# Second cross attention of a Perceiver block: where head values, output product and absorbed queries stand in a round

## What is computed

```python
def _L1_xattn_ref(x, context, Wq, Wk, Wv, Wo, bo):
...
    B, Sq, _ = x.shape
    h, d = (HEADS, DIM_HEAD)
    scale = d ** (-0.5)
    q = (x @ Wq).reshape(B, Sq, h, d).transpose(0, 2, 1, 3)
    k = (context @ Wk).reshape(B, -1, h, d).transpose(0, 2, 1, 3)
    v = (context @ Wv).reshape(B, -1, h, d).transpose(0, 2, 1, 3)
    scores = jnp.einsum('bhid,bhjd->bhij', q, k) * scale
    attn = jax.nn.softmax(scores, axis=-1)
    out = jnp.einsum('bhij,bhjd->bhid', attn, v)
    out = out.transpose(0, 2, 1, 3).reshape(B, Sq, h * d)
    return out @ Wo + bo
...
x = x + _L1_xattn_ref(_layernorm(x, axis=-1), ctx_768, L1_xattn_Wq, L1_xattn_Wk, L1_xattn_Wv, L1_xattn_Wo, L1_xattn_bo)
```

## Time and profile before

| | us |
|---|---|
| three executions | 2245.73, 2248.62 (median), 2255.6 |
| the profiled execution | 2261.09 |
| its span, first to last instruction | 2259.3 |
| mean granted clock of PE, of 2.4 GHz | 0.905 |
| second cross attention, rounds | some 1008 to 1788 |

### The profile page before, as it was taken

The page is one execution under the profiler, slowest core; times in us unless marked ns, Lnnn a source line. Parts: engine busy times, 40 slices in busy tenths (PEclk is TensorE's granted clock), DMA queues, the critical chain, the costliest instruction groups (busy, mean ns, idle before and its releaser), DMA issues.

```text
span 2259.3 us, 43825 instructions
## 1 busy us (share of the span) xinstructions
PE 2044.9 (91%) x17873; PEld 1683.2 (75%) x17873; DVE 1324.7 (59%) x2900; ACT 923.9 (41%) x1868; POOL 651.6 (29%) x674
## 2 busy tenths in 40 slices
PE   6999999999995887759999999999999899879994
PEld 4777777777774776659898988989889667646663
DVE  5787777877877555437564755756455245532222
ACT  4666666666554333524343433434333221102221
POOL 4444444444434220233232323323231000020002
PEclk9999999999997989779899998999889765579997
DMA  6111111111002000132122311223110230030102
GB/s 196 46 31 51 40 31 45 47 31 38 25 2 86 0 1 1 45 84 72 52 58 60 88 52 52 52 52 103 52 52 1 107 152 1 10 152 24 33 29 68
DMA packets 55735, 119.80 MB, mean 53 GB/s; under 512 B 4321, under 2 KB 41905, under 8 KB 54001
## 3 DMA queue, kind: packets, MB, share of 16 engines
q1 hardware_dynamic: 54000, 112.80, 16.9%
q0 software_dynamic: 1536, 4.20, 0.6%
HBM read 107.80 MB, written 9.18 MB: 52 GB/s over the span
## 4 chain that ended last, share of the span: by engine, by line
PE 73%; DVE 13%; ACT 4%; issue 4%; DMA 3%; POOL 1%; SPq 0%; POOLq 0%; ACTq 0%; DVEq 0%
PE ps L104 13%; PE ps L163 6%; PE ps L1944 5%; PE ps L433 5%; PE ps L472 5%; PE ps L1285 4%; DVE arena L531 4%; PE ps L456 3%; DMA wsb<-in_ctxT 3%; PE ps L1286 3%; PE ps L1968 3%; PE ps L450 2%; PE ps L1272 1%; PE ps L1271 1%; PE ps L1275 1%
## 5 line engine op out<-in xcount | busy, mean ns | idle before, releaser
L531 DVE TENSOR_REDUCE arena<-ps 128x1 f32<-128x400 f32 (+1 forms) x512 | 258.2, 566 | 137.2 <-PE ps L433 137.2
L651 ACT ACTIVATE arena<-ps 128x384 f32<-128x384 f32 (+1 forms) x512 | 223.4, 523 | 102.4 <-PE ps L456 102.4
L1285 PE MATMUL ps<-arenaR 128*128 128x386 f32 x768 | 240.5, 352 | 1.1 <-DVE arenaR L1365 1.1
L1286 PE MATMUL ps<-arenaR 128*128 128x256 f32 x768 | 217.8, 284 | 0.0
L1507 POOL TENSOR_TENSOR arenaR<-h,arenaR 128x400 fp32r<-128x400 f32 (+1 forms) x60 | 57.9, 965 | 448.0 <-ACT arenaR L1450 442.5
L557 DVE TENSOR_TENSOR arena<-arena 128x512 f32<-128x512 f32 x192 | 176.5, 919 | 5.1 <-ACT arena L651 1.5
L1465 ACT CAST arenaR<-ps 128x512 fp32r<-128x512 f32 (+1 forms) x256 | 116.5, 508 | 144.7 <-PE ps L163 141.7
L709 POOL TENSOR_TENSOR arena<-arena 128x512 f32<-128x512 f32 (+1 forms) x96 | 134.0, 1396 | 101.7 <-ACT arena L651 99.4
L1365 DVE TENSOR_TENSOR arenaR<-ps,arenaR 128x512 fp32r<-128x512 f32 (+1 forms) x256 | 138.5, 582 | 19.4 <-ACT arenaR L1465 17.4
L1285 PEld LDWEIGHTS ps<-arenaR 128*128 128x128 f32 x768 | 147.4, 192 | 1.9 <-DVE arenaR L1365 1.4
L1286 PEld LDWEIGHTS ps<-arenaR 128*128 128x128 f32 x768 | 148.1, 193 | 0.4
(11 more groups left out here) (307 smaller groups left out, 4839.2 us busy)
## 6 DMA issues: line engine op xcount, KB each, us to landing
wsb<-in_ctx SPq DMA_DIRECT2D x16, 1152.0 KB
arena<-in_ctxT SPq DMA_DIRECT2D x16, 800.5 KB, 5.2
arena<-in_ctxT SPq DMA_DIRECT2D x32, 400.2 KB, 7.3
wsb<-in_ctxT SPq DMA_DIRECT2D x32, 400.2 KB, 7.5
gu<-in_m_gu SPq DMA_DIRECT2D x8, 1536.0 KB, 21.1
h<-in_ctxT SPq DMA_DIRECT2D x15, 800.5 KB, 5.1
dn<-in_m_dn SPq DMA_DIRECT2D x8, 768.0 KB, 9.6
xs_rows<-zeros SPq DMA_DIRECT2D x1, 2944.0 KB, 15.9
```

What stands on the lines that cost most here:

```text
L531: e.tensor_reduce(mx4[n % 2][:, u, i:i + 1], ps[:, at("look", n, i, u), 0:400 + (i == 3)], AX.X, ALU.max).then_inc(c.maxed.at((n, i, u)), 1)
L651: e.activation(v[:, u, 0:128 * GN[s]], ps[:, at("st", n, s, u), 0:128 * GN[s]], ACT.Exp).then_inc(c.exp_a.at((x0, n, s, u)), 1)
L1285: e.matmul(o, PTh[:, t, :], v[:, t, 0:386], start=(t == 0), stop=False)
L1286: e.matmul(o[:, 0:256], PTl[:, t, :], v[:, t, 0:256], start=False, stop=False)
```

## The change

- Head values are made one pair at a time: `head_values(tile, g)`, 4 products into the first 128 columns of bank 7, followed by an ACT copy of 128 x 128 into `aT[:, g, :]`. It stands on PE between two halves of `values(n-1)`, in each of the four rounds after the odd batch's pair has been transposed.
- The output product (`project`, now only 4 products) comes one round later, at the start of the round.
- `absorb(b+1, j)` moves from the end of the round to between `scores(n, 1)` and `turn_p(n-1, 2)`, on DVE to between the second maximum and the third `p_low`, on ACT to between the second and the third `p_high`. Its waits are the same.
- The wait of DVE's `turn` for the head values of the tile before is now per pair. SP and POOL are unchanged. The loop has one round more (N + 2), so that the last `turn` and head values stand in it.

```diff
+    def has_values(n):
+
+        m = n - 2
+        return (m // NP // 2, m % NP) if m >= 0 and m // NP % 2 == 1 else None
+
+    def projects(n):
+
+        m = n - 3
+        return m // NP // 2 if m >= 0 and m % NP == NP - 1 and m // NP % 2 == 1 else None
+
+    def asks(n):
+
+        b = n // NP + 1
+        return b // 2 if n % NP == 0 and b < NB and b % 2 == 0 else None
...
-        def values(n):
+        def values(n, half):
             o, v = ps[:, 6, 0:386], cN[n // NP % 2]
-            w.wait_ge(*c.p_lo((x1, n, 3)))
-            if n:
-                w.wait_ge(*c.o_norm((x1, n - 1)))
-            w.wait_ge(*cn_made((n // NP, 3)))
-            w.wait_ge(*c.dv("x1 pads"))
-            for t in range(KT - 1):
+            if half == 0:
+                w.wait_ge(*c.p_lo((x1, n, 3)))
+                if n:
+                    w.wait_ge(*c.o_norm((x1, n - 1)))
+                w.wait_ge(*cn_made((n // NP, 3)))
+                w.wait_ge(*c.dv("x1 pads"))
+            for t in range(6) if half == 0 else range(6, KT - 1):
                 e.matmul(o, PTh[:, t, :], v[:, t, 0:386], start=(t == 0), stop=False)
                 e.matmul(o[:, 0:256], PTl[:, t, :], v[:, t, 0:256], start=False, stop=False)
-            t = KT - 1
-            e.matmul(o[:, 0:256], PTl[0:KL, t, :], v[0:KL, t, 0:256], start=False, stop=False)
-            e.matmul(o, PTh[0:KL, t, :], v[0:KL, t, 0:386], start=False, stop=True).then_inc(c.summed.at((x1, n)), 1)
+            if half == 1:
+                t = KT - 1
+                e.matmul(o[:, 0:256], PTl[0:KL, t, :], v[0:KL, t, 0:256], start=False, stop=False)
+                e.matmul(o, PTh[0:KL, t, :], v[0:KL, t, 0:386], start=False, stop=True).then_inc(c.summed.at((x1, n)), 1)
...
+        def head_values(tile, g):
+
+            w.wait_ge(*o_take((2 * tile + 1) * NP + g))
+            w.wait_ge(*bank7[0])
+            pairs = []
+            for i in range(g * hpg, (g + 1) * hpg):
+                pairs += [(W["wv1"][:, i, :], oT1[:, i, :]), (W["wv2"][0:64, i, :], oT2[0:64, i, :])]
+            mm(e, ps[:, 7, 0:128], pairs).then_inc(va_made.at((tile, g)), 1)
+            bank7[0] = c.a_out((x1, tile, g))
+
         def project(tile):
-            w.wait_ge(*o_take((2 * tile + 2) * NP - 1))
+            w.wait_ge(*c.a_out((x1, tile, G - 1)))
             w.wait_ge(*bank7[0])
-            for g in range(G):
-                pairs = []
-                for i in range(g * hpg, (g + 1) * hpg):
-                    pairs += [(W["wv1"][:, i, :], oT1[:, i, :]), (W["wv2"][0:64, i, :], oT2[0:64, i, :])]
-                p = mm(e, ps[:, 7, 128 * g:128 * g + 128], pairs)
-            p.then_inc(va_made.at(tile), 1)
-            w.wait_ge(*c.a_out((x1, tile)))
...
-        for n in range(N + 1):
+        for n in range(N + 2):
             b, j = n // NP, n % NP
-            if n < N and j == 0 and b + 1 < NB and (b + 1) % 2 == 0:
-                queries((b + 1) // 2)
-            if n >= 1:
+            if projects(n) is not None:
+                project(projects(n))
+            if asks(n) is not None:
+                queries(asks(n))
+            if 1 <= n <= N:
                 turn_p(n - 1, 0)
                 turn_p(n - 1, 1)
             if n < N:
                 scores(n, 0)
                 scores(n, 1)
-            if n >= 1:
+                if b + 1 < NB:
+                    absorb(b + 1, j)
+            if 1 <= n <= N:
                 turn_p(n - 1, 2)
                 turn_p(n - 1, 3)
             if n < N:
@@ -1331,13 +1355,12 @@
                 scores(n, 3)
             if n >= 2:
                 turn(n - 2)
-                if (n - 2) % NP == NP - 1 and (n - 2) // NP % 2 == 1:
-                    project((n - 2) // NP // 2)
-            if n >= 1:
-                values(n - 1)
-            if n < N and b + 1 < NB:
-                absorb(b + 1, j)
-        turn(N - 1)
+            if 1 <= n <= N:
+                values(n - 1, 0)
+            if has_values(n):
+                head_values(*has_values(n))
+            if 1 <= n <= N:
+                values(n - 1, 1)
...
-                w.wait_ge(*va_made(b // 2 - 1))
+                w.wait_ge(*va_made((b // 2 - 1, j)))
...
             if n < N:
                 maximum(n, 0)
                 maximum(n, 1)
-            if n >= 1:
+                if b + 1 < NB:
+                    absorb(b + 1, j)
+            if 1 <= n <= N:
                 p_low(n - 1, 2)
                 p_low(n - 1, 3)
             if n < N:
...
-        def project(tile):
-            w.wait_ge(*va_made(tile))
+        def head_values(tile, g):
+            w.wait_ge(*va_made((tile, g)))
             if tile:
                 w.wait_ge(*c.projected((x1, tile - 1)))
-            e.copy(flat(aT), ps[:, 7, 0:128 * G]).then_inc(c.a_out.at((x1, tile)), 1)
+            e.copy(aT[:, g, :], ps[:, 7, 0:128]).then_inc(c.a_out.at((x1, tile, g)), 1)
...
-            if n >= 1:
-                for g in range(4):
-                    p_high(n - 1, g)
+            if 1 <= n <= N:
+                p_high(n - 1, 0)
+                p_high(n - 1, 1)
+            if n < N and b + 1 < NB:
+                absorb(b + 1, j)
+            if 1 <= n <= N:
+                p_high(n - 1, 2)
+                p_high(n - 1, 3)
             if n < N:
...
-            if n >= 2 and (n - 2) % NP == NP - 1 and (n - 2) // NP % 2 == 1:
-                project((n - 2) // NP // 2)
-            if n < N and b + 1 < NB:
-                absorb(b + 1, j)
-        project(NT - 1)
+            if has_values(n):
+                head_values(*has_values(n))
```

More of the change, by code:

```diff
@@ L1554, in over @@
         w.wait_ge(*c.dv(("moments", x1, NT - 1)))
-        w.wait_ge(*c.a_out((x1, NT - 1)))
+        w.wait_ge(*c.a_out((x1, NT - 1, G - 1)))
         w.wait_ge(*cn_made((NB - 1, 3)))
```

## The result

The changed kernel takes 2309.68 us (median of 4, 2309.2 to 2310.47) against 2252.11 (median of 4, 2245.73 to 2256.12): ratio 1.026, interval 1.023 to 1.029. It is slower by 58 us on the medians and by 48 us between the two profiled executions (2309.2 and 2261.09). The forecast was 2296 in 2270 to 2360, and 2308 for the profiled execution.

The account below looks back on a forecast made before the run. TensorE was taken to bound plain rounds, so its waits are paid in full. The profiled 2261.1 + 115 (wait) + 3 (POOL) - 71 (gain) gives 2308; less 12.5 for the median, 2296 us, range 2270 to 2360.

Parts of the forecast that it names:

- The wait in 59 rounds: In rounds 1 to 59 TensorE waits 1.95 us because the moved `absorb` copy waits for its own round's scores: 115 us added.
- S: The end of a round's last score matmul on TensorE, 1137.31 us in the profiled round; the added wait was counted from it.
- What the change takes away: At `project`, queries and transposes: 9.7 us per eight rounds, 68 for seven periods, plus 3 at the end: 71 us.
- the rest is slow clock: Remainder of the 9.7 us a period after waits before queries (1.37), at `project` (1.03 + 0.68) and before transposes (1.1).
- the late context load: Cause given for the wait before transposes, 1.1 us a period; a longer round was to give the load more time.
- the forecast's own case: The forecast without any rival, chance 0.60: wait 111 to 121, gain 60 to 78, POOL 0 to 28, so 2282 to 2330.
- POOL's blocks: In a batch's first round `absorb` waits 0.2 us for POOL's block-diagonal queries, 14 times: 3 us added, between 0 and 28.
- The clock: Assumption that TensorE's fast clock survives the new waits, since it stayed 1.00 around one wait of 1.87 us.
- the wait is not there: Rival, chance 0.06: the `absorb` copy runs at once, only the gain is left, 2181 us.
- gain and wait cancel: Rival, chance 0.05: the last five probability tiles pass on sooner, wait 1.2 us a round, within 11 us of 2248.6.
- the gain is given back in part: Rival, chance 0.07: POOL's blocks cost the full 28 us, or a late context load stays: 2320 us.
- the clock falls at the new waits: Rival, chance 0.22: the fast clock is lost after many new waits, 1.65 us each: 2345, up to 2393 us.

## Why the prediction was right

**The wait in 59 rounds**, with 1.07 us ahead of the transposes and 0.45 ahead of the value products where 1 and 1 were named, was worked out as 1.95 us from rows of a kernel that did not have it, and is 1.96. It holds since each link was an instruction that the trace already showed, and since the question asked of the moved copy was not how long it takes but what it waits for and what is queued behind it. The links came out as 0.09, 0.27, 1.50 and 0.06 us, so only the hand-over from PE to ACT was off, by 0.05. The run with the needless wait kept shows that it is this wait alone. The two idle times in the rows add up to 1.52 only, since they are counted from the drained ends; the values start 1.95 later than before, counted from S (S + 1.92 against S - 0.03), and that is what a round pays.

**What the change takes away** was 71 us. The run without the wait but with all the rest gives 2250.55 - 2185.89 = 65, and + 3 for POOL was in the sum, so 68 was to be seen. The terms: the period of eight rounds came out 0.2 us from the working, and 0.4 in the run without the wait; the 1.37 us before queries went; the head pairs show no wait; ACT's copies were hidden. What the sum called "the rest is slow clock" (9.7 less the three waits, 5.5 us a period) was not looked into there; the run with the other order of products has now shown it to be worth 26 us on the medians and 46 between the profiled executions. One reason was wrong though its term came true: the late context load was to vanish since it gets more time in a longer round. With two buffers the rounds are no longer than before and the eight of a period even shorter (87 us), and yet ACT waits for these loads 0.6 us in all instead of 12.1. Why the load is in time there was not tried.

**Where the sum was lucky.** It has + 47 us and the profiled executions differ by 48, but not by its terms alone. The first `turn` before, in the changed kernel and with two buffers:

```profile
1030.05 0.38 PE L163 MATMUL ps<-ident,arena 128*128 128x128 f32 x2
1039.50 0.41 PE L163 MATMUL ps<-ident,arena 128*128 128x128 f32 x2 [1.07 <-DVE arenaR L1381]
1030.22 0.38 PE L163 MATMUL ps<-ident,arena 128*128 128x128 f32 x2
```

The wait costs 9.3 us ahead of it, where the sum has one round, 1.95. It took round 0 to be free since it has no values, but the copies of round 0 wait as well, and in round 1 PE then waits 3.9 us for the exponentials (2.2 before) and 1.9 for the lower parts. These 7.5 us that no term had are offset by 3 us in the seven periods that follow (41 more than before, where the terms give 44) and by 3.5 us behind them. The stated upper bound of the forecast's own case was added up wrongly as well: 2248.6 + 121 + 28 - 60 is 2338 and not 2330.

**POOL's blocks** cost 3 us as forecast (two rounds of each eight are 0.2 and 0.3 us longer than the wait makes them), but only since a head pair or queries stood ahead. Without a head pair they cost 11 to 12.5 us, within the bound of 28.

**The clock** was the weak step. The forecast took the fast clock from one wait of 1.87 us, and called that side harmless. It was right for the changed kernel, but with a margin of less than 0.27 us of wait, which nothing in the prediction showed: the wait of 1.87 us stood once, and the new one comes in each round. That the clock held is in part luck. The rival's price of 1.65 us for a shortest low stretch was a little high; it is 1.4. The Trainium skill ("TensorE: Matmul & The Clock Gate", section "A second HAM failure mode: psum-queue depth-cycling") has a clock that swings when TensorE idles a little between groups again and again. At waits of 1.96 us a round the trace does not agree (1.00 throughout), with 0.27 us more it does (25 low stretches).

**Rivals.** That the wait is not there is excluded by the row of L1480; that gain and wait cancel, or that the gain is given back in part, by the time and the terms above; that the clock falls at the new waits, by the windows, though the two runs with a longer wait show it. The forecast for the median (2296) was 14 us low since it subtracted the 12.5 us by which the profiled execution of before lay above its median; the changed kernel's executions all lie within 1.3 us of each other, its profiled one at 2309.2. The kernel before spreads over 10 us, and its slower executions tend to have the lower granted clock (0.902 at 2263.51 us, 0.913 at 2239.80, behind the runs on one chip), so this spread is at least in part clock. The difference of two single executions (48 us) and that of the medians (58 us) are therefore both readings of the same change.

## What to carry to other kernels

When an instruction moves up its engine's queue, look up what it waits for and whether that has happened by then; all that is queued behind it inherits the wait. Here the fix was a second buffer of 8 KB a partition, which turns the change from + 58 us to - 65 us, and with the products of equal row count side by side to - 73 us, the fastest version of this study. A regular wait of PE can have a price beyond its length: here 0.27 us more in each round cost 16 us by itself and 36 us by the clock.

## What the runs showed of the hardware

- Products that change between 128 and 64 rows at each step take 0.208 us an instruction at the upper clock, in pairs of equal rows 0.16, where queries of 128 rows throughout take 0.12 (1.89 us for 16). At a change of rows the weight load starts 0.20 us behind the start of the matmul ahead of it, otherwise 0.002.
- The clock's fall is steep in the length of a repeated wait: none at the regular waits of 1.96 us from round 2 on, 25 low stretches with 2.23 us, 51 with 2.77. A microsecond at the low clock cost 0.4 us in these rounds.
